# A two-layer decoder step with a routed expert stage: the expert blocks listed in three parts, eleven pairs of blocks run beside the last batch's routing, ten result buffers

## What is computed

```python
x = x + _L1_xattn_ref(_layernorm(x), ctx_512, ...)      # causal cross attention, 16 heads of 16
x = x + _L1_ffn_ref(_layernorm(x), gate, w_gate, w_up, w_down)

# _L1_ffn_ref: E = 28 experts, M = 176, TOP_K = 6
scores = jax.nn.softmax(x @ gate_weight.T)
topk_w, topk_idx = jax.lax.top_k(scores, TOP_K)
topk_w = topk_w / (topk_w.sum(-1) + 1e-20)
for each expert e:
    h = silu(x @ w_gate[e]) * (x @ w_up[e])
    y = y + w_tok[:, None] * (h @ w_down[e])      # w_tok is 0 where e was not chosen
```

## Time and profile before

| | before |
|---|---|
| time, median of 3 runs | 819.01 us (817.14 to 819.1) |
| span of the profiled execution | 814.3 us |
| what lies around the span, median minus span | 4.7 us |
| busy: PE / DVE / ACT / POOL | 692.1 / 471.8 / 374.6 / 286.4 us |
| chain that ended last, by line | PE L804 28%, PE L812 7%, POOL xg L2650 3% |

### The profile page before, as it was taken

The page is one execution under the profiler, slowest core; times in us unless marked ns, Lnnn a source line. Parts: engine busy times, 40 slices in busy tenths (PEclk is TensorE's granted clock), DMA queues, the critical chain, the costliest instruction groups (busy, mean ns, idle before and its releaser), DMA issues.

```text
span 814.3 us, 15589 instructions
## 1 busy us (share of the span) xinstructions
PE 692.1 (85%) x5126; PEld 472.4 (58%) x5134; DVE 471.8 (58%) x1367; ACT 374.6 (46%) x1024; POOL 286.4 (35%) x277
## 2 busy tenths in 40 slices
PE   8999999999879988798988999698435999999960
PEld 5667677777535766687756766465322555555530
DVE  2466668788867535546664755344440566665654
ACT  2464655556411502545557467436012555655520
POOL 3043435454410002212310302413462456556651
PEclk9999999999999999979997999859557999999985
DMA  8999999001150034313000018100293678777857
GB/s 323 290 350 350 350 349 370 6 2 48 68 212 35 0 123 129 107 37 104 27 27 1 1 45 343 63 21 35 94 401 97 122 142 150 145 143 148 149 93 240
DMA packets 86061, 116.89 MB, mean 144 GB/s; under 512 B 8348, under 2 KB 77277, under 8 KB 84958
## 3 DMA queue, kind: packets, MB, share of 16 engines
q1 hardware_dynamic: 69964, 97.57, 36.8%
q0 software_dynamic: 11168, 14.75, 10.4%
q10 hardware_dynamic: 4850, 3.57, 1.6%
HBM read 59.82 MB, written 56.04 MB: 142 GB/s over the span
## 4 chain that ended last, share of the span: by engine, by line
PE 35%; issue 6%; POOL 4%; DVE 3%; DMA 3%; ACT 2%; SPq 1%; ACTq 1%; another core or an unknown queue 0%; POOLq 0%; DVEq 0%
PE PS L804 28%; PE PS L812 7%; POOL xg L2650 3%; DMA y<-fwd 2%; ACTq L2515 1%; ACT ws L2193 0%; SPq L751 0%; DVE R L1932 0%; POOL R L2639 0%; DMA W_all<-y 0%; DVE R L1939 0%; SPq L739 0%; ACT R L2465 0%; DVE R L1985 0%; DMA xg<-xr,pos 0%
## 5 line engine op out<-in xcount | busy, mean ns | idle before, releaser
L804 PE MATMUL PS<-R 32*128 32x128 f32 (+11 forms) x1196 | 157.2, 387 | 18.8 <-issue 11.2
L804 PEld LDWEIGHTS PS<-R 32*128 32x128 f32 (+5 forms) x1196 | 95.6, 194 | 58.6 <-issue 41.4
L2669 POOL DMA_INDIRECT y<-fwd x62 | 96.6, 1557 | 89.2 <-DVE fwd L2158 52.2
L804 PE MATMUL PS<-W_all,fgu 128*64 x372 | 108.9, 443 | 6.7 <-DVE fgu L2143 1.9
L2193 ACT ACTIVATE R<-PS 128x512 f32<-128x512 f32 (+5 forms) x164 | 80.4, 539 | 63.2 <-PE PS L812 42.6
L804 PE MATMUL PS<-ws,fgu 128*64 128x352 f32 (+1 forms) x372 | 109.0, 443 | 0.0
L812 PE MATMUL PS<-ident,R 128*128 128x128 f32 x600 | 92.4, 296 | 10.6 <-POOL R L2639 3.9
L812 PEld LDWEIGHTS PS<-ident,R 128*128 128x128 f32 x600 | 72.2, 154 | 36.1 <-issue 21.3
L804 PEld LDWEIGHTS PS<-W_all,fgu 128*64 128x64 f32 x372 | 48.9, 138 | 55.6 <-issue 16.0
L2193 ACT ACTIVATE ws<-W_all 128x960 f32 x62 | 58.8, 996 | 38.3 <-issue 37.1
L2586 POOL TENSOR_TENSOR rs<-rs,mh 128x1 f32<-128x1 f32 x48 | 27.0, 563 | 111.4 <-DVE rs L1569 111.1
(11 more groups left out here) (295 smaller groups left out, 1450.9 us busy)
## 6 DMA issues: line engine op xcount, KB each, us to landing
xg<-zrow SPq DMA_DIRECT2D x28, 1088.0 KB, 12.4
W_all<-in_wgu SPq DMA_DIRECT2D x2, 3360.0 KB
W_all<-in_wgu SPq DMA_DIRECT2D x1, 6720.0 KB
xh<-xg SPq DMA_DIRECT2D x72, 68.0 KB
y<-zrow SPq DMA_DIRECT2D x2, 2304.0 KB, 16.1
R<-in_wqkv SPq DMA_DIRECT2D x1, 4096.0 KB, 21.2
xT<-xg SPq DMA_DIRECT2D x50, 68.0 KB
scrq<-bqkv SPq DMA_DIRECT2D x12, 256.0 KB, 2.9
```

Source lines behind the costliest of these rows:

```text
L804: return e.matmul(out, l, r, start=start, stop=stop, skip_group_check=True)
L2669: e.indirect_dma_start(out=D[f"y{y}"][0:to, :], out_offset=bass.IndirectOffsetOnAxis(ap=toi[j % 3][rows, :], axis=0), in_=ys[j % 3][rows, ...
```

## The change

- The block list is made in three parts. `mn`, `mc`, `ms` replace `mp`, each three times: part 0 after batches 0 and 1 (pairs 0 to 4), part 1 after batch 2 (pairs 5 to 10), part 2 after batch 3 (pairs 11 to 30). Parts 0 and 1 list full groups of 64 tokens alone, `mpn[:, 6:7]` carries how many groups of an expert are already listed.
- The pieces of the first pairs are written into the orders among the last batch's routing, on all five engines. `warm` is gone.
- `ys` has 10 buffers. The accumulators and `ACC` are the same.
- So that the expert stage may begin while the cross attention still has its data, the last batch's q, k, v, probabilities and transposes have places of their own (`late`, `F`, `zrow`), `W_all` is loaded in three steps that wait for earlier pieces, and the row buffers of a pair are loaded when DVE has read the old rows, no longer when the add has landed.

```diff
-ACC = [j % NY for j in range(NB - 3)] + [1, 1, 1]
+ACC = [j % 2 for j in range(NB - 3)] + [1, 1, 1]
+FIRST = (0, 5, 11, NPAIR)
...
     "POOL": (
-        "sc.0.1 sc.0.2 sc.0.3 sc.1.0 rt_stat.2 sc.1.1 sc.1.2 sc.1.3 sc.2.0 sc.2.1 rt_stat.3 sc.2.2 sc.2.3 "
-        "sc.3.0 sc.3.1 sc.3.2 sc.3.3 "),
+        "sc.0.1 sc.0.2 sc.0.3 sc.1.0 rt_stat.2 sc.1.1 sc.1.2 sc.1.3 sc.2.0 sc.2.1 rt_stat.3 hm sc.2.2 sc.2.3 "
+        "ed.0 sc.3.0 sc.3.1 ed.1 sc.3.2 sc.3.3 ed.2 ed.3 "),
...
     def experts():
-        add("mp", banks=[0, 1, 7])
-        for q in range(-3, 0):
-            add("ld", q)
...
-        for q in range(NPAIR + 1):
+        for q in range(5, NPAIR + 1):
             if q + 2 < NPAIR:
                 add("ld", q)
...
             def ld(q):
+                p, w = q + 3, q + 2
+                if p < NPAIR:
...
+                    if p in FIRST:
+                        for b in range(turn(p) + 2):
+                            e.wait_ge(sem(f"xg{b}"), 16 * 12)
+                        e.wait_ge(sem("blocks"), turn(p) + 1)
...
             def ld_w(g):
-                u = fill(*(("ao_m", 3), ("xe_m", 3))[g])
-                e.wait_ge(u.full, u.f + 1)
-                for a, z in (((0, 7), (21, NE)), ((7, 21),))[g]:
-                    experts_(a, z, sem(f"w{g}"))
+                u = fill(*(("ao_m", 3), ("xpv", 15), ("xe_t", 2, 1))[g])
+                e.wait_ge(u.full, u.f + 1)
+                for a, z in (((0, 7), (21, NE)), ((7, 16),), ((16, 21),))[g]:
+                    experts_(a, z, sem("w"))
...
             def et(j):
                 u = fill("et", j)
                 if j == 0:
-                    e.wait_ge(sem("blocks"), 1)
-                    room(u)
-                    e.wait_ge(sem("hm0"), 2)
-                    warm(u.t[:, :], 22)
+                    e.wait_ge(sem("w"), 64)
...
             def ed(q):
-                    if j >= 3:
-                        e.wait_ge(sem(f"y{ACC[j - 3]}"), 16 * (NTH[j - 3] + 1))
+                    if j >= NYS:
+                        e.wait_ge(sem(f"y{ACC[j - NYS]}"), 16 * (NTH[j - NYS] + 1))
```

More of the change, by code:

```diff
@@ L42, in blocks_of, with turn @@
     return [2 * p, 2 * p + 1]
+def turn(p):
+    return sum(p >= f for f in FIRST[1:-1])
 def half(h):
@@ L566, in program @@
         OTx = view(fwd_, 512, 2, 256)
[L567 to L570, removed]
+        mxx = [few[:, 8 * i:8 * i + 8] for i in range(3)]
+        rcx = view(few, 24, 2, 16)
         c1 = Carve(R1, 2400)
@@ L591, in program @@
         ejb = c1(NB)
-        mpn, mpt, mpb = c1(4, parts=28), c1(16, parts=28), c1(2 * NB, parts=28)
-        mpr = c1(2 * NB, parts=1)
+        mpn, mpt, mpb = c1(10, parts=28), c1(16, parts=28), [c1(80, parts=28) for _ in range(2)]
+        mpr = c1(80, parts=1)
         def groups(b, part, rows):
@@ L731, in ld @@
             def ld(q):
[L733 to L736, removed]
-                    e.wait_ge(sem("blocks"), 1)
[L738 to L745, removed]
+                p, w = q + 3, q + 2
+                if p < NPAIR:
+                    for name, args, at in (("xp_tr", (3,), 0), ("rt_g", (2,), 3), ("xpv", (31,), 5)):
+                        if p == at:
+                            u = fill(name, *args)
+                            e.wait_ge(u.full, u.f + 1)
[3 more added lines that the diff above has]
+                        e.wait_ge(sem("blocks"), turn(p) + 1)
+                    n = nc.values_load_multi_w_load_instructions(
+                        blocks[0:1, AT_SP + 6 * p:AT_SP + 6 * p + 4], engines=(mybir.EngineType.SP,), min_val=0, max_val=PAD,
+                        skip_runtime_bounds_check_because=bound)[1]
+                    for i, j in enumerate(blocks_of(p)):
@@ L746, in ld @@
                         if j >= NX:
-                            i = j - NX
-                            e.wait_ge(sem(f"y{ACC[i]}"), 16 * (NTH[i] + 1))
+                            u = fills("ed", (j - NX) // 2)[j % 2]
+                            e.wait_ge(u.free, u.k + 1)
                         for h in range(2):
-                            src = D["xg"][bass.ds(n[2 * (j % 2) + h], 64), :]
+                            src = D["xg"][bass.ds(n[2 * i + h], 64), :]
                             e.dma_start(xb[j % NX][half(h), :], src).then_inc(sem(f"xb{j % NX}"), 16)
[L752 to L755, removed]
+                if w >= 0:
+                    if w == 0:
+                        u = fill("xp_q", 3, 1)
+                        e.wait_ge(u.full, u.f + 1)
+                    elif w < 3:
+                        u = fill("xpv", 31)
+                        e.wait_ge(u.full, u.f + 1)
+                    else:
+                        for u in fills("ed", w - 3):
@@ L2447, in xp_q @@
             def xp_q(b, g):
-                s = b % 2
                 u = fill("xp_q", b, g)
+                if b == 3 and g == 0:
+                    w = fill("ao_m", 3)
+                    e.wait_ge(w.full, w.f + 1)
                 if b >= 2 and g == 0:
@@ L2507, in wc @@
                 if q == 0:
-                    e.wait_ge(sem("blocks"), 1)
-                    e.wait_ge(sem("w0"), 32)
-                    e.wait_ge(sem("w1"), 16)
+                    e.wait_ge(sem("w"), 64)
+                    u = fill("xpv", 31)
+                    e.wait_ge(u.full, u.f + 1)
+                if q in FIRST:
+                    e.wait_ge(sem("blocks"), turn(q) + 1)
                 if q >= 3:
@@ L2522, in wc @@
                     e.dma_start(w2[q % 3][64:112, h, :], D["wd2"][bass.ds(r, 48), :]).then_inc(sem(f"w2_{q % 3}"), 16)
-            def ldb():
-                for b in range(4):
-                    e.wait_ge(sem(f"xg{b}"), 16 * 12)
-                n = nc.values_load_multi_w_load_instructions(
-                    blocks[0:1, AT_SP + 2:AT_SP + 4], engines=(mybir.EngineType.Activation,), min_val=0, max_val=PAD,
-                    skip_runtime_bounds_check_because="VectorE took the minimum with this bound")[1]
-                for h in range(2):
-                    e.dma_start(xb[1][half(h), :], D["xg"][bass.ds(n[h], 64), :]).then_inc(sem("xb1"), 16)
             def et(q):
@@ L2634, in l1_init @@
                     e.memset(p30[i][:, 29:30], 3.0).then_inc(sem("l1_set"), 1)
+                e.wait_ge(sem("init"), 16 * (NE + 1 + NY))
+                for c in range(2):
+                    e.memset(va[3][c][:, :, 16:17], 1.0).then_inc(sem("l1_set"), 1)
             def un(i):
```

249 lines of the change are left out of this document (158 added, 91 removed), and 20 rows, old and new, of the table ORDERS.

## The result

The changed kernel takes 808.59 us (median of 4 runs, 807.03 to 811.92) against 818.08 us (4 runs, 816.02 to 819.1): a ratio of 0.9862, 95% interval [0.9819, 0.9905]. The forecast was 805.3 us.

A forecast was written before the change was run, and what follows sets the result against it. PE's hole of some 30 us before the experts, then PE's pace; afterwards the accumulator adds bind. Block 5's add at 636.1 plus 138.2 and the last steps gives 787.1, 13.7 us earlier: 819.0 - 13.7 = 805.3 us, range 790 to 816.

The forecast's parts named there:

- The early start: Front of the expert stage: pair 0 at about 583 us, PE starting 40 us earlier, nothing charged for weight loads.
- The last batch's routing: Routing before batch 3's scatters: slowed by expert work, 2 + 2.5 + 8.4 + 1.3 us, `pos` at 615.3 (606 to 625).
- POOL's queue: POOL behind `pos`: twelve scatters, pair 1's adds and pair 2's first add put block 5's add at 636.1 us.
- Ten buffers: "so PE never stops": Expert results: ten buffers let DVE be five pairs (25 us) ahead, so PE never stops; three would have stopped it.
- They become the bound: Expert stage: adds, spread behind the scatters, become the bound; last add at 787.1 against 800.8 us.
- 5.12 us a step: Adds on accumulator 1 from block 5: 27 steps to block 59 at 5.12 us, bounds 4.81 and 5.4.
- The sign that the prediction had named: End of the expert stage: PE's last matmul some 20 us before the last add but two.
- 26 of 40: Expert stage: of the 40 us that PE gains, 26 are given back because the adds become the bound.
- Rival A: Expert stage: PE stays the bound, its last pair setting the end; -32 us, 787 us; chance 0.1.
- Rival D: Cross attention: the three lists' steps delay it, another low-clock stretch costs some 10 us; no change; chance 0.05.
- B: Last batch's routing: PE stays at 1.2 GHz until `rk.3`, `pos` near 623; 813 us; chance 0.13.
- C: Adds on POOL: slower steps, gain gone at 5.63 us, 830 us at 6.02; chance 0.07.

The follow-up runs named there:

- the kernel with all batches paced: Changed kernel with batch 0's scatters one at a time and those of batches 1 to 3 in groups of three, each awaiting earlier landings: 792.7 us, ratio 0.9700.
- the paced kernels: Changed kernel with scatters waiting for earlier landings: batches 0 to 2 so limited 794.6 us, batch 0 alone 795.7 us, all four batches 792.7 us.
- 803.3 us: Kernel before the change with one edit, each scatter of batch 0 waiting for the landing of the one before: 803.3 us, ratio 0.9805.
- the routing first: Changed kernel, last batch's routing ahead of expert pieces, six of its scatters before pair 0's adds: 803.4 us; with scatters in flight limited to (1, 6, 3, 3): 786.7 us.
- the fastest kernel: Changed kernel with the last batch's routing before expert pieces and scatters in flight limited to 1, 6, 3, 3 for batches 0 to 3: 786.7 us, ratio 0.9586.

## Why the prediction was right, and where it was right for a wrong reason

The forecast of 805.3 us was 3.5 us under the profiled execution: 6.1 at the last add and 0.3 behind it, less 2.85 around the span (1.85 us against 4.7). That closeness is in part luck. The forecast's times count from the kernel before, whose first scatter starts 3.3 us later. Counted from the first scatter, the last add was forecast at 293.1 us and came at 302.6: of a gain of 13.7 us on this stretch 9.4 did not come. The 9.4 are 4.2 in the routing, 1.2 in POOL's queue, 3.8 in the first two steps of the adds and 0.7 in the other 25, less 0.5 in the last two.

- **The early start** held: pair 0 starts at 579.3 (forecast 583; its own terms, 575.8 and 5.5, give 581.3). The weight and row loads there cost nothing that shows.
- **The last batch's routing** seemed to hold, `pos` at 616.0 against 615.3, but it was mis-sized. From the first scatter to `pos` it is 125.5 us against 107.2 before, so 18.4 more and not the 14.2 that I had charged to expert pieces in the way. In the trace two stops of PE lie between pair 0 and the marks, 5.27 us to 593.03 and 4.89 to 599.01, around batch 2's scatters, 10.2 us that no term holds. The kernel before idles there too (4.99 us to 591.05, 3.28 to 598.04), so how much of the 18.4 is theirs stays open. With the pieces put behind the routing, `pos` still came only at 608.
- **POOL's queue** held: block 5's add is 22.0 us behind `pos`, forecast 20.8.
- **Ten buffers: "so PE never stops"** failed. PE stopped for 5.60 us until 638.91, and the first two steps behind block 5 took 6.62 and 7.37 us; they are 3.8 of the 9.4 us. Results were not three pairs ahead of the adds: block 4's was written at 635.56 and its add issued at 636.33, and three buffers do as well.
- **"They become the bound"** failed as the cause, though not as a number. I forecast 5.12 us a step for 27 steps, and 25 steps from 652.23 to 780.91 measured 5.15. But four accumulators leave that as it is, and two accumulators manage 4.97 in the kernel with all batches paced: 5.12 was no floor of the adds. It was read from adds that ran beside PE, and so it was PE's own pace, gaps included, as much as the adds'. Three of the four rows shown were released by adds, but over all 62 adds of the kernel before more of the idle time ended with DVE than with an add:

```profile
  DVE fwd L2158: 52.2, 26
  DMA y<-fwd: 27.4, 17
```

  The sign that the prediction had named says the same: PE's last matmul was to come some 20 us before the add of block 59, and it ends at 782.7, 1.8 us behind that add's start. The adds kept up with PE.
- **Where PE's 44 us went** (579.3 instead of 623.3): PE's last matmul ends at 782.7 instead of 790.1, so 7.4 are left. Not the adds took the 36 us back, as I wrote of 26 of 40. By block 10's add (655.29 against 662.91) the lead has already shrunk to 7.6, so all of it is lost in front of pair 5. But little of it was PE's time to gain, since the kernel before did the last batch's routing and the 22 warming matmuls in its hole. This is the stretch of the kernel before that starts level with the new one (579.3 and the 3.3 us of its later start) and ends at the same place of the work (650.0 and the lead of 7.6):

```profile
582.60:657.60 75.00, 47.65 (x283) 26.15 (x283) 26.13 (x107) 22.68 (x40) 36.88 (x36) 0.75 0.64 197
```

  In those 75.0 us PE is busy for 47.7 at a clock of 0.75 and idle for 27.4; in the 70.7 us of the kernel after it is busy for 48.9 at 0.76 and idle for 21.8. The change has spread the work over the hole, but four fifths of the idle time are still there and the clock is no higher. Of the 21.8 the four stops (5.27, 4.89, 3.20, 5.60) make 19.
- **Rival A** (PE is the bound, 787 us) named the right engine and the wrong price: 32 us of gain, with no stops and no low clock in it. Pacing gives most of its gain in the cross attention, where the kernel before has it too, so the paced kernels are to be held against 803.3 us: they gain 7.5 to 10.6 us, and 16.6 with the routing first, and not 32. **Rival D** had the place of the stops ("another such stretch costs some 10 us"), but made the lists' steps on DVE their cause; it measured 15, and the cause was on POOL. **B** and **C** did not happen: the slow clock stayed within the forecast's bounds, and the mean of the 27 steps was 5.28.

**What stays open.** What in a run of scatters holds PE's signals up. The trace does not prove whether PE's results or only their signals are late, since the ends of matmuls are modelled; but the signal of pair 2's down projection came at 635.29, when PE had long begun the next pieces (627.45 to 633.1). Batch 0's first three scatters, alone at 494 us in the kernel before, harm nothing; batch 2's first six already do (DVE 4.56 us to 590.84); adds in pairs show nothing of the kind (from 640 to 780 us no signal of PE there is more than 0.5 us late). Groups of three that alternate with adds still leave one wait of 4.82 us (ACT, to 618.65, in the fastest kernel). Whether the count of rows in flight decides, the count of scatters or POOL's gaps, these runs do not separate, since pacing changes all three.

## What to carry to other kernels

When several engines wait at once for something that the trace says was finished long ago, look at what POOL is sending at that moment, and try the same indirect transfers a few at a time: that edit of two lines was worth more here (13 to 17 us) than the change under study (8 to 10 by the medians). A pace that is measured on a consumer running beside its producer may be the producer's until a run with more room (here four accumulators) shows otherwise. And when a stage can start earlier, work out what it will stand beside in its new place, and compare stretches that hold the same work: of PE's 44 us 7.4 were left, and PE was busy as long and at the same clock as before in front of pair 5.

## What was not expected of the hardware

- Nine indirect scatters of 128 rows in a row on POOL (0.96 us each, 1.26 apart) left DVE waiting 5.50 us and PE idle for 5.53 us; one at a time they left no such wait. The late signals were PE's alone (up to 6.84 us; the other engines' under 0.02). In bytes a seventeenth made no difference (6.92 us).
- PE idle for 5.5 us at 520 us was followed by about 25 us at 1.2 GHz under work that otherwise runs at 2.4; the stop cost 15 us in all, three times its length.
- An indirect add of 128 rows of 1 KB took 3.7 to 5.8 us to land after its issue (the last chain shown), on a mean step of 5.2 us with two accumulators in flight.
